# Fifteen shared units among the convolution steps, fourteen ahead of the experts, eleven behind them

## The chip, the core and the metric

The kernel runs on one core of one Trainium2 chip. The metric is device time in microseconds (us) of one execution. TensorE (PE) multiplies, VectorE (DVE), ScalarE (ACT) and GpSimd (POOL) do the rest of the arithmetic, and SyncE (SP) issues most transfers. The program is written in blocks, one for each engine: each engine does its instructions in the order in which its block has them, and semaphores tie the blocks together.

## What is computed

x is 16 x 128 x 256. A layer with a long convolution (gated by `ctx_2048`) adds to x, then a mixture of 32 experts (4 for each token, with a shared expert beside them) adds to the sum. Cut to its core:

```python
x = x + tanh(g_xattn) * xattn(ctx, ctx, layernorm(x))    # kv = k_i * v_j by head; y = conv(kv, ssm_kernel) + D*kv; out = sum_i y * q_i
inp = layernorm(x)
xn = w_norm * rmsnorm(inp)                               # 2048 tokens x 256
probs = softmax(xn @ w_router); w_topk, sel = top_k(probs, 4)
buf[e, pos] = xn[token]                                  # up to 128 rows for each of 32 experts
y = (silu(buf @ w_gate) * (buf @ w_up)) @ w_down         # inner width 176
out[token] += y[e, pos] * w_topk
sh = silu(xn @ sw_gate) * (xn @ sw_up) @ sw_down         # the shared expert, inner width 704
out = out + sigmoid(xn @ w_shared_gate) * sh
x = x + tanh(g_ffn) * (inp + out)
```

## The kernel before, in words

**Stages.** The 16 sequences are worked on in 4 groups of 4 (`G`, `GB`). The convolution of a group takes 8 steps (`NP_`, two heads each): VectorE and POOL form products, TensorE convolves (`conv`, L1040), VectorE multiplies and reduces (`mult`, `reduce`, L788). While the steps of group g run, the tokens of group g-1 get their norm, router logits, top 4 and slots, a chain through TensorE (`out_tr`, `xn_transposes`, `logits`, `rank`), ScalarE (`token_rows`, `xn_evac`, `lg_copy`, `exps`, `token_coef`, `base_rows`) and VectorE (`x1`, `token_stats`, `token_shift`, `top`, `top_masks`, `token_slots`, `token_gates`). POOL then sends the rows of the tokens to their experts' buffers (L396, 64 sends). The chain of the last group has no convolution beside it; it is written out by itself on every engine. When all rows are sent, SyncE loads the experts' inputs (L313); the 32 experts follow (TensorE L1204 to L1255, with ScalarE and VectorE between its products); POOL adds their results into three sums in DRAM (L470). In the tail SyncE loads the sums, VectorE adds them to `x_sb` (`add_sum`, L987 to L1018, 24 additions of 128 x 512), and ScalarE's queue stores the output.

**Shared units.** The shared expert of the 4 groups is cut into 40 units (`unit(n)`, L1101), 10 for a group: 5 full units (`gate`, `up`, six products of 128 x 512 each), one remainder (`gate` alone, six products, since 704 is 5 times 128 and 64 more) and 4 downs (`down`, L1086, six products each of 128 x 256). Unit n is number n % 10 of group n // 10: 0 to 4 are full, 5 is the remainder, 6 to 9 are downs. A unit of the first two kinds needs a `silu` on ScalarE (L538) and a `use` on VectorE (L791: the product of the two halves, L798 or L800), and a down needs only a `use` (L806: it adds to `x_sb`). There are single PSUM tiles `pg` and `pu` for them: the next gate waits for the silu before, the next up for the use before, and a down of number 2 or 3 for the use of an earlier down. The first gate of a group waits for the uses of all downs of the group before it, and for the low part of the group's tokens (`xnT_low`). The first down of a group waits for the use of its remainder.

**Where the units stand.** Units 0 to 17 stand among the convolution steps, by the table `UNIT_AT` (L45): unit `UNIT_AT[g, p]` comes on TensorE behind the convolution of step (g, p+1), on ScalarE at step (g, p) (behind `token_rows` of p = 2, behind the first `xn_evac` of p = 3, between `lg_copy` and `exps` of p = 4), and its use on VectorE ahead of the reduction of step (g, p). `LATE = 18` (L48) is the first of the units ahead of the experts: 18 to 31 stand in the last chain and behind it (TensorE L1191 to L1202, ScalarE L664 to L674, VectorE L943 to L960). `UNITS_END = range(32, 40)` (L50) are those behind the experts. On VectorE their uses are woven into the tail: in a loop of four one `add_sum` of sum 2, a use, another `add_sum` (L1002 to L1005), then the 16 additions of sums 0 and 1 (L1011 to L1018), then the four last uses.

## Time and profile before

| | before |
|---|---|
| median of 3 runs | 321.08 us (318.03, 321.08, 321.09) |
| profiled execution | 319.66 us, its span 317.9 us |
| PE busy | 275.6 us, 87% |
| PEld (weight loads, beside PE) busy | 224.8 us, 71% |
| DVE busy | 204.1 us, 64% |
| POOL busy | 192.0 us, 60% |
| ACT busy | 122.7 us, 39% |

The busy shares are averages over the span. The kernel has stages with different limits (to 78 us loads and the first two groups, to 158 us groups 2 and 3, to 206 us the last chain and the sends, to 287 us the experts, then the tail), so a share says little of what an edit in one stage is worth. The chain that ended last names, for each piece of the time, the engine or transfer that was waited for; the timeline of an engine gives the start and length of each run of equal instructions and, in brackets, how long the engine was idle just before and what ended that wait; the windows give busy time and the granted TensorE clock (PEclk, 1.00 is 2.4 GHz, 0.50 is 1.2 GHz) of a stretch.

### The profile page before, as it was taken

What the parts mean: (1) busy time and instruction counts of PE and PEld (TensorE: products, weight loads), DVE (VectorE), ACT (ScalarE), POOL (GpSimd) and SP (SyncE); (2) the same over time, 40 slices, a digit from 0 to 9 for tenths busy, and PEclk for the clock granted to TensorE, in tenths of its full rate; (3) what the DMA queues carried; (4) which work ended last, traced back from release to release, by engine and by line L of the source; (5) the groups of instructions that cost most, each with busy time, mean ns of one, the idle gap of its engine ahead of it and who ended that gap; (6) DMA issues with size and microseconds to landing.
All of it is one profiled execution on the core that took longest, in us unless ns stands there. A gap on an engine that the chain in (4) does not pass through costs nothing.

```text
span 317.9 us, 4992 instructions
## 1 busy us (share of the span) xinstructions
PE 275.6 (87%) x1482; PEld 224.8 (71%) x1482; DVE 204.1 (64%) x586; ACT 122.7 (39%) x342; POOL 192.0 (60%) x265
## 2 busy tenths in 40 slices
PE   2978659947998989899699999899999999999980
PEld 1877549835887868798477777677777777778750
DVE  2679999747769998688953621134554445555695
ACT  2248436871365701349115920143334333321100
POOL 2898977535689867686377677107655666652200
PEclk9979997968999999999979999999999999999996
DMA  6899999998112112011059930409999999668798
GB/s 203 246 301 292 302 269 386 384 299 234 56 42 72 61 53 74 37 65 45 4 174 284 236 102 0 132 20 241 252 260 259 256 290 295 104 114 234 165 354 306
DMA packets 53322, 59.65 MB, mean 188 GB/s; under 512 B 6744, under 2 KB 48920, under 8 KB 53296
## 3 DMA queue, kind: packets, MB, share of 16 engines
q1 hardware_dynamic: 42336, 47.24, 48.9%
q0 software_dynamic: 7680, 8.95, 14.3%
q10 hardware_dynamic: 3280, 3.15, 2.9%
q8 instruction: 12, 0.20, 0.2%
q14 instruction: 14, 0.11, 0.1%
HBM read 36.83 MB, written 27.21 MB: 201 GB/s over the span
## 4 chain that ended last, share of the span: by engine, by line
PE 42%; DVE 18%; SPq 15%; DMA 12%; ACT 6%; issue 5%; POOL 1%; DVEq 0%; ACTq 0%; POOLq 0%
PE Y L1220 12%; DMA arena<-in_ctx_dram 5%; SPq L300 5%; PE pg L1065 5%; DVE arena L788 4%; PE pd L1239 4%; DMA expert_sum<-arena,ide 4%; PE Y L1239 4%; SPq L290 4%; SPq L296 3%; PE pu L1065 3%; DVE x_sb L989 3%; PE Y L1211 2%; PE pm L1230 2%; PE pg L1098 2%
## 5 line engine op out<-in xcount | busy, mean ns | idle before, releaser
L396 POOL DMA_INDIRECT dispatched<-rows,dsu x64 | 63.4, 990 | 31.5 <-issue 23.9
L470 POOL DMA_INDIRECT expert_sum<-arena,ide x32 | 49.6, 1550 | 46.8 <-DVE arena L979 39.2
L788 DVE TENSOR_REDUCE arena<-arena 128x128 f32<-128x1024 f32 x32 | 38.7, 1212 | 0.2
L1053 PE MATMUL Y<-arena 128*128 128x144 f32 x128 | 28.3, 304 | 11.5 <-DVE arena L780 11.0
L966 DVE TENSOR_TENSOR arena<-arena,Y 128x176 f32<-128x176 f32 x32 | 10.8, 338 | 37.6 <-ACT arena L688 37.6
L798 DVE TENSOR_TENSOR act<-silu,pu 128x512 f32<-128x512 f32 x20 | 13.7, 686 | 31.5 <-PE pu L1065 17.5
L1053 PEld LDWEIGHTS Y<-arena 128*128 128x128 f32 x128 | 20.8, 196 | 15.8 <-issue 12.3
L681 ACT ACTIVATE arena<-Y,wn 128x128 f32<-128x128 f32 x64 | 20.0, 364 | 29.6 <-PE Y L1211 29.5
L547 ACT ACTIVATE silu<-pg 128x512 f32<-128x512 f32 x20 | 11.9, 595 | 48.9 <-PE pg L1065 48.8
L1055 PE MATMUL Y<-arena 128*128 128x144 f32 x128 | 26.7, 291 | 0.0
L1054 PE MATMUL Y<-arena 128*128 128x144 f32 x128 | 26.7, 291 | 0.0
L1065 PE MATMUL pg<-xnT_high,swgu_high 128*128 128x512 f32 x48 | 20.9, 435 | 5.8 <-ACT silu L547 5.0
L1220 PE MATMUL Y<-arena 128*128 128x352 f32 x72 | 24.3, 460 | 0.0
L1098 PE MATMUL pu<-swd,act 128*128 128x256 f32 (+1 forms) x84 | 21.8, 403 | 0.0
L1098 PE MATMUL pg<-swd,act 128*128 128x256 f32 (+1 forms) x84 | 21.2, 393 | 0.0
L1054 PEld LDWEIGHTS Y<-arena 128*128 128x128 f32 x128 | 20.7, 196 | 0.0
L1055 PEld LDWEIGHTS Y<-arena 128*128 128x128 f32 x128 | 20.6, 195 | 0.0
L384 POOL TENSOR_TENSOR arena<-arena 128x256 f32<-128x256 f32 x32 | 20.5, 642 | 0.0
L1065 PE MATMUL pg<-xnT_high,swgu_low 128*128 128x512 f32 x48 | 19.3, 402 | 0.0
L1065 PE MATMUL pg<-xnT_low,swgu_high 128*128 128x512 f32 x48 | 19.2, 401 | 0.0
L1220 PE MATMUL Y<-first_slots,arena 128*128 128x352 f32 x56 | 18.9, 460 | 0.0
L1098 PEld LDWEIGHTS pu<-swd,act 128*128 128x128 f32 (+1 forms) x84 | 15.6, 198 | 4.5 <-issue 2.7
(180 smaller groups left out, 653.3 us busy)
## 6 DMA issues: line engine op xcount, KB each, us to landing
expert_sum<-zrow SPq DMA_DIRECT2D x3, 2176.0 KB, 17.5
dispatched<-zrow SPq DMA_DIRECT2D x1, 4624.0 KB, 21.1
arena<-dispatched SPq DMA_DIRECT2D x32, 144.5 KB, 4.1
arena<-expert_sum SPq DMA_DIRECT2D x16, 256.0 KB, 5.8
arena<-in_L_ffn_w_gate_dram SPq DMA_DIRECT2D x18, 176.0 KB, 3.7
arena<-in_L_ffn_w_up_dram SPq DMA_DIRECT2D x18, 176.0 KB, 4.7
arena<-in_L_ffn_w_down_dram SPq DMA_DIRECT2D x18, 176.0 KB
first_slots<-in_L_ffn_w_gate_dram SPq DMA_DIRECT2D x14, 176.0 KB, 4.0
```

The source lines that it names most:

```text
L384: pool.tensor_tensor(o[:, :, :, 5:9], k[:, :, 0:4].rearrange("m e (u t) -> m e u t", t=1).broadcast_to([P, 16, 4, 4]), k[:, :, 4:8].rearra ...
L396: pool.indirect_dma_start(buf, bass.IndirectOffsetOnAxis(ap=dsu[:, t % 2, j:j + 1], axis=0), rows[:, t % 2, j // K, :], None, bounds_check ...
L470: pool.indirect_dma_start(accs[a], bass.IndirectOffsetOnAxis(ap=ide[:, e % NO:e % NO + 1], axis=0), ye[:, e % NO, :], None, compute_op=ALU ...
L681: ins = act_e.activation(xeT[:, e % 2, c, :], xt_out(e)[:, c * P:(c + 1) * P], ACT.Copy, scale=wn[:, c:c + 1])
L788: dve.tensor_reduce(oT[:, g % 2, :, 2 * HD * p:2 * HD * (p + 1)].rearrange("l e (a j) -> l a e j", a=2), Z[:, p % 2].rearrange("l (a e) j ...
L1053: pe.matmul(yv[:, 0], TT[:, h, P:L], kvv[:, 0], start=True, stop=True)
L1054: pe.matmul(yv[:, 1], TT[:, h, 0:P], kvv[:, 0], start=True, stop=False)
L1055: ins = pe.matmul(yv[:, 1], TT[:, h, P:L], kvv[:, 1], start=False, stop=True)
L1065: ins = pe.matmul(out_, swgu[a][:, c, col:col + P], xnT[b][:, gs % 2, c, :], start=(k == 0), stop=(k == n - 1))
L1098: ins = pe.matmul(down_out(gs, b), act[0:w, j, b * S:(b + 1) * S], swd[0:w, j, :], start=(j == 0), stop=(j == NJ - 1))
L1220: ins = pe.matmul(gu_out(e), xeT[:, e % 2, c, :], wgu[slot_of(e)][:, :, c, :], start=(c == 0), stop=(c == 1))
L1239: ins = pe.matmul(y_out(e), aeT[:, e % 2, c, :], wd[slot_of(e)][:, c, :], start=(c == 0), stop=(c == 1))
```

## The change

The table has units 0 to 14 at steps (2, 1) to (3, 7) in place of 0 to 17 at (1, 6) to (3, 7). `LATE` is 15, and `UNITS_END` is 29 to 39. So three units leave the convolution steps, and these are, in number, two downs and one remainder; the 14 units ahead of the experts are now 15 to 28 (a remainder and four downs of group 1, the whole of group 2 but its last down), and 29, a down of group 2, stands behind the experts with all ten of group 3. In the last chain ScalarE does the silu of unit 15 ahead of the token rows, and `last_exps` comes at once behind `lg_copy`, where a silu stood between; VectorE's uses there are of the remainder and of downs; TensorE no longer puts gates and ups between the transposes, the logits and the rank, but downs. In the tail, VectorE uses unit 29 first, then does the pairs of sum 2 with the uses of 30 to 33 behind each pair, then the uses of 34 and 35, then the 16 additions and the last four uses.

```diff
--- before.py
+++ after.py
@@ -42,12 +42,11 @@
 LN_EPS, RMS_EPS = 1e-5, 1e-6
 
 
-UNIT_AT = {(1, 6): 0, (1, 7): 1,
-           (2, 0): 2, (2, 1): 3, (2, 2): 4, (2, 3): 5, (2, 4): 6, (2, 5): 7, (2, 6): 8, (2, 7): 9,
-           (3, 0): 10, (3, 1): 11, (3, 2): 12, (3, 3): 13, (3, 4): 14, (3, 5): 15, (3, 6): 16, (3, 7): 17}
-LATE = 18
+UNIT_AT = {(2, 1): 0, (2, 2): 1, (2, 3): 2, (2, 4): 3, (2, 5): 4, (2, 6): 5, (2, 7): 6,
+           (3, 0): 7, (3, 1): 8, (3, 2): 9, (3, 3): 10, (3, 4): 11, (3, 5): 12, (3, 6): 13, (3, 7): 14}
+LATE = 15
 WARM = 10
-UNITS_END = range(32, 40)
+UNITS_END = range(29, 40)
 
 
 def flamingo_block(nc, x, ctx_in, g_xattn, g_ffn, ssm_kernel, ssm_D, w_norm, w_router, w_gate, w_up,
@@ -658,16 +657,14 @@
                             q_stats(g + 2)
 
             t = G - 1
+            silu(LATE)
             token_rows(t)
             xn_evac(t, 0)
             xn_evac(t, 1)
-            silu(LATE + 2)
             lg_copy(t)
+            last_exps(t)
             for c in range(2):
                 xn_high(t, c)
-            silu(LATE + 3)
-            last_exps(t)
-            silu(LATE + 4)
             token_coef(t)
             base_rows(t)
             for n in range(LATE + 5, UNITS_END[0]):
@@ -948,12 +945,12 @@
             use(LATE)
             token_shift(t)
             use(LATE + 1)
+            use(LATE + 2)
             top(t)
             shift(t)
             top_masks(t)
-            use(LATE + 2)
+            use(LATE + 3)
             token_slots(t)
-            use(LATE + 3)
             token_gates(t)
             last_low(t)
             for k in range(LATE + 4, UNITS_END[0]):
@@ -997,12 +994,15 @@
                 if e + 1 < E:
                     e_aT(e + 1)
                 e_yout(e)
+            use(UNITS_END[0])
             dve.wait_ge(s["base_ready"], G)
             dve.wait_ge(s["down_used"], GB * (G - 1))
             for k in range(G):
                 pair_mark[0, 2 * k] = mark(add_sum(2, 2 * k))
-                use(UNITS_END[k])
                 pair_mark[0, 2 * k + 1] = mark(add_sum(2, 2 * k + 1))
+                use(UNITS_END[k + 1])
+            for k in UNITS_END[G + 1:-GB]:
+                use(k)
 
             def add_first(i):
                 after(pair_mark[0, i])
@@ -1190,14 +1190,12 @@
             out_tr(t, 1)
             unit(LATE)
             unit(LATE + 1)
+            unit(LATE + 2)
             xn_transposes(t, 0)
             xn_transposes(t, 1)
-            gate(2, 0)
             logits(t)
-            up(2, 0)
-            gate(2, 1)
+            unit(LATE + 3)
             rank(t)
-            up(2, 1)
             for n in range(LATE + 4, UNITS_END[0]):
                 unit(n)
```

The first place is ScalarE at the end of group 1 and the start of group 2 (`vq`, `rqs`, `nbq` are the query's coefficients, `arena` the queries and keys of later steps, `silu` the unit's result out of `pg`). Before:

```order
L521 ACTIVATE vq<-qss 128x4
L547 ACT_TABLE_LOAD
L547 ACTIVATE silu<-pg 128x512
L525 ACTIVATE rqs<-rq 128x4
L527 ACTIVATE nbq<-nmq,rq 128x1 x4
L499 ACTIVATE arena<-x_sb,nbq,rqs 128x2x128
L547 ACTIVATE silu<-pg 128x512
L484 ACTIVATE arena<-pd 128x2x8x16
L492 ACTIVATE arena<-pd 128x2x16x8
L499 ACTIVATE arena<-x_sb,nbq,rqs 128x2x128
L547 ACTIVATE silu<-pg 128x512
L484 ACTIVATE arena<-pd 128x2x8x16
```

Now:

```order
L520 ACTIVATE vq<-qss 128x4
L524 ACTIVATE rqs<-rq 128x4
L526 ACTIVATE nbq<-nmq,rq 128x1 x4
L498 ACTIVATE arena<-x_sb,nbq,rqs 128x2x128
L483 ACTIVATE arena<-pd 128x2x8x16
L491 ACTIVATE arena<-pd 128x2x16x8
L498 ACTIVATE arena<-x_sb,nbq,rqs 128x2x128
L483 ACTIVATE arena<-pd 128x2x8x16
L491 ACTIVATE arena<-pd 128x2x16x8
L498 ACTIVATE arena<-x_sb,nbq,rqs 128x2x128
L546 ACT_TABLE_LOAD
L546 ACTIVATE silu<-pg 128x512
```

The silus of units 0, 1 and 2 stood between the coefficients and the queries and keys of the group, with the table load of the first; now the first silu, unit 0's, comes behind four query and key steps.

The second place is VectorE in the last chain (`x_sb<-pu` and `x_sb<-pg` are uses of downs, `act` a use of a full unit or of the remainder, `mx` to `M` the top 4, `rk` the first step of the slots). Before:

```order
L838 TENSOR_SCALAR vs<-mv 128x4
L806 SCALAR_TENSOR_TENSOR x_sb<-pu,sgf,x_sb 128x256
L844 SCALAR_TENSOR_TENSOR nb<-mv,rs 128x4
L806 SCALAR_TENSOR_TENSOR x_sb<-pg,sgf,x_sb 128x256
L852 MAX mx<-lg 128x8 x4
L870 TENSOR_TENSOR ex<-lg,mx 128x128
L859 COPY top<-mx 128x4x4
L861 MATCH_REPLACE left<-top,lg 128x36 x4
L866 TENSOR_TENSOR M<-left,lg 128x128
L798 TENSOR_TENSOR act<-silu,pu 128x512
L897 TENSOR_TENSOR rk<-pm,carry 128x128
```

Now:

```order
L835 TENSOR_SCALAR vs<-mv 128x4
L797 TENSOR_TENSOR act<-silu,pg 64x512
L841 SCALAR_TENSOR_TENSOR nb<-mv,rs 128x4
L803 SCALAR_TENSOR_TENSOR x_sb<-pu,sgf,x_sb 128x256
L803 SCALAR_TENSOR_TENSOR x_sb<-pg,sgf,x_sb 128x256
L849 MAX mx<-lg 128x8 x4
L867 TENSOR_TENSOR ex<-lg,mx 128x128
L856 COPY top<-mx 128x4x4
L858 MATCH_REPLACE left<-top,lg 128x36 x4
L863 TENSOR_TENSOR M<-left,lg 128x128
L803 SCALAR_TENSOR_TENSOR x_sb<-pu,sgf,x_sb 128x256
L894 TENSOR_TENSOR rk<-pm,carry 128x128
```

The use of the remainder is new in this place, ahead of `nb`, and a use of a down (`x_sb<-pu`, unit 18) stands where the use of a full unit (`act`, unit 20) stood, ahead of the slots.

The third place is VectorE in the tail (`x_sb<-x_sb,arena` are the additions of the sums, `act` the uses of full units and, 64 wide, of the remainder; the rest are uses of downs). Before:

```order
L989 TENSOR_TENSOR x_sb<-x_sb,arena 128x512
L798 TENSOR_TENSOR act<-silu,pu 128x512
L989 TENSOR_TENSOR x_sb<-x_sb,arena 128x512 x2
L798 TENSOR_TENSOR act<-silu,pu 128x512
L989 TENSOR_TENSOR x_sb<-x_sb,arena 128x512 x2
L798 TENSOR_TENSOR act<-silu,pu 128x512
L989 TENSOR_TENSOR x_sb<-x_sb,arena 128x512 x2
L800 TENSOR_TENSOR act<-silu,pg 64x512
L989 TENSOR_TENSOR x_sb<-x_sb,arena 128x512 x17
L806 SCALAR_TENSOR_TENSOR x_sb<-pu,sgf,x_sb 128x256
L806 SCALAR_TENSOR_TENSOR x_sb<-pg,sgf,x_sb 128x256
L806 SCALAR_TENSOR_TENSOR x_sb<-Y,sgf,x_sb 128x256 x2
```

Now:

```order
L803 SCALAR_TENSOR_TENSOR x_sb<-pg,sgf,x_sb 128x256
L986 TENSOR_TENSOR x_sb<-x_sb,arena 128x512 x2
L795 TENSOR_TENSOR act<-silu,pu 128x512
L986 TENSOR_TENSOR x_sb<-x_sb,arena 128x512 x2
L795 TENSOR_TENSOR act<-silu,pu 128x512
L986 TENSOR_TENSOR x_sb<-x_sb,arena 128x512 x2
L795 TENSOR_TENSOR act<-silu,pu 128x512
L986 TENSOR_TENSOR x_sb<-x_sb,arena 128x512 x2
L795 TENSOR_TENSOR act<-silu,pu 128x512 x2
L797 TENSOR_TENSOR act<-silu,pg 64x512
L986 TENSOR_TENSOR x_sb<-x_sb,arena 128x512 x16
L803 SCALAR_TENSOR_TENSOR x_sb<-pu,sgf,x_sb 128x256
```

A use of a down has come ahead of the first addition, two more uses of full units lie ahead of that of the remainder, and all sums but the first eight additions are behind it (16 now, 17 before).

## Rows read from the trace of the kernel before

**Rows 1.** Page, chain that ended last: shares of the span by engine

```profile
PE 42%; DVE 18%; SPq 15%; DMA 12%; ACT 6%; issue 5%; POOL 1%; DVEq 0%; ACTq 0%; POOLq 0%
```

**Rows 2.** Chain of waits to 78 us: start, us, what

```profile
69.92 8.07 DMA arena<-in_ctx_dram
```

**Rows 3.** Windows: stretch, length, busy us (instructions) by engine, PEclk, DMA share, GB/s

```profile
78.00:120.00 42.00, 39.61 (x247) 33.86 (x248) 34.82 (x95) 18.71 (x49) 33.22 (x53) 1.00 0.17 60
...
158.00:206.00 48.00, 45.00 (x209) 34.73 (x210) 18.32 (x62) 15.91 (x34) 31.08 (x31) 0.96 0.56 151
```

**Rows 4.** Timeline of PE, 60 to 130 us: start, us, what, [idle before, releaser]

```profile
68.31 0.79 PE L1065 MATMUL pg<-xnT_high,swgu_high 128*128 128x512 f32 x1 [4.18 <-ACT silu L547]
...
73.53 0.41 PE L1053 MATMUL Y<-arena 128*128 128x144 f32 x2
...
78.04 0.44 PE L1031 MATMUL pd<-ident,arena 128*128 128x128 f32 x2 [1.72 <-DMA arena<-in_ctx_dram]
...
78.46 0.48 PE L1065 MATMUL pg<-xnT_high,swgu_high 128*128 128x512 f32 x1
...
81.29 0.60 PE L1117 MATMUL pm<-ident,arena 128*128 128x128 f32 x4
...
96.93 0.48 PE L1053 MATMUL Y<-arena 128*128 128x144 f32 x2 [1.20 <-DVE arena L780]
...
118.14 0.48 PE L1053 MATMUL Y<-arena 128*128 128x144 f32 x2 [1.14 <-DVE arena L780]
```

**Rows 5.** Timeline of PE, 130 to 208 us

```profile
158.71 1.10 PE L1117 MATMUL pm<-ident,arena 128*128 128x128 f32 x4 [2.57 <-DVE arena L788]
...
200.39 0.47 PE L1065 MATMUL pg<-xnT_high,swgu_high 128*128 128x512 f32 x1 [0.81 <-DVE x_sb L806]
...
205.97 0.39 PE L1211 MATMUL Y<-ident,arena 128*128 128x128 f32 x2
```

**Rows 6.** Timelines of POOL, DVE and SP's queue, 70 to 202 us

```profile
74.37 1.22 POOL L396 DMA_INDIRECT dispatched<-rows,dsu  x1 [5.37 <-issue]
...
179.79 1.33 POOL L396 DMA_INDIRECT dispatched<-rows,dsu  x1 [1.58 <-DVE rows L888]
...
175.46 0.29 DVE L897 TENSOR_TENSOR rk<-pm,carry 128x128 f32<-128x128 f32 x1 [0.27 <-PE pm L1147]
...
178.98 1.29 DVE L876 TENSOR_TENSOR xnT_low<-xnT,xnT_high 128x512 fp32r<-128x512 f32 x2
...
201.50 12.39 SPq L313 DMA_DIRECT2D arena<-dispatched  x9
```

**Rows 7.** Timeline of all engines in the tail, 278 to 318 us

```profile
287.05 0.59 PE L1065 MATMUL pg<-xnT_high,swgu_high 128*128 128x512 f32 x1
...
289.98 0.39 PE L1065 MATMUL pg<-xnT_high,swgu_high 128*128 128x512 f32 x1
...
295.42 0.39 PE L1065 MATMUL pg<-xnT_high,swgu_high 128*128 128x512 f32 x1
...
296.79 2.94 PE L1098 MATMUL pu<-swd,act 128*128 128x256 f32 x12
...
297.62 0.69 DVE L800 TENSOR_TENSOR act<-silu,pg 64x512 f32<-64x512 f32 x1
...
301.12 2.04 DVE L989 TENSOR_TENSOR x_sb<-x_sb,arena 128x512 f32<-128x512 f32 x3 [2.09 <-DMA arena<-expert_sum]
...
303.41 9.53 DVE L989 TENSOR_TENSOR x_sb<-x_sb,arena 128x512 f32<-128x512 f32 x13 [0.25 <-DMA arena<-expert_sum]
...
312.97 0.48 DVE L806 SCALAR_TENSOR_TENSOR x_sb<-pu,sgf,x_sb 128x256 f32<-128x256 f32 x1
```

**Rows 8.** Windows of 1 us around 68 and 159: columns as in rows 3

```profile
68.00:69.00 1.00, 0.69 (x2) 0.60 (x3) 0.71 (x2) 1.00 (x6) 1.00 (x3) 0.50 0.91 252
...
159.00:160.00 1.00, 1.00 (x6) 1.00 (x5) 0.20 (x2) 0.00 (x0) 0.94 (x1) 0.50 0.18 56
```

## Prediction, made before the changed kernel ran

> **What bounds the kernel now.** I read the chain that ended last first: TensorE has the largest share, VectorE less than half of that, and SyncE's queue and the transfers about a quarter together [rows 1]. So no engine is the bound throughout, and I went on by stages, with cuts where the chain changes hands.
>
> To 78.0 us the chain is SyncE's queue and then one transfer, the context of the last group, which TensorE waits for at 78.04 [rows 2, 4]. Nothing that is computed before that sets the end. From 78 to 158.7 (groups 2 and 3 of the convolution) TensorE is busy 39.6 of the first 42 us [rows 3]; its few waits are for VectorE [rows 4], which was itself held by a use that came behind ScalarE's token rows. From 158.7 to 206.0 two paths run side by side and end together: POOL's 32 row sends with the first expert load behind them (201.50), and TensorE's shared units; TensorE is busy 45.0 of 48 us and starts the experts at 205.97, at once after its last unit [rows 3, 5, 6]. The experts follow at TensorE's pace to 287.05. In the tail TensorE has four gate/up units and four downs left, but VectorE has the last word: it ends its uses at 298.3, adds one piece, then waits 2.09 us for the expert sums, and adds 16 pieces from 301.12 to 312.94 with hardly a gap [rows 7].
>
> **Prices.** A full unit (gate and up, 12 products) takes 2.72 us (289.98 to 295.42 is two), the remainder unit 1.37, a down product 2.94 [rows 7]. A use is 0.6 to 0.7 us, after a down 0.5.
>
> **The work that moves.** The convolution steps lose one remainder and two downs: 7.3 us. Ahead of the experts two full units go and one down and one remainder come: 1.1 us less. Behind them two full units and one down come: 8.4 us more. The count is the same in all, so only what each stage does with its share matters.
>
> *Up to 78 us: nothing, and a price.* Units 0 and 1 stood ahead of 73.5 [rows 4]. Without them the end of this stage is still the transfer. But TensorE then has only one convolution step and the first transposes of group 1's output left. VectorE, no longer held by unit 0, hands these over some 5 us earlier (as long as POOL now waits for VectorE's slots at 74.37 [rows 6]), so TensorE has nothing from about 69 to 78. What that does to its clock is in the rows: after 4.18 us of waiting the granted clock was 0.50 (1.2 GHz), and the unit that began at 68.31 took 5.2 us to the next instruction, against 2.83 at 78.46 [rows 4, 8]. After 2.57 us of waiting at 158.71 the clock was again 0.50 [rows 5, 8], while the unit behind the 1.72 us of 78.04 ran at full pace [rows 4]. With 9 us idle I expect 1.2 GHz at 78, for about as long as from 68.31 on: 2.3 us lost, the 5.2 less 2.8. Bounds: 0 if it recovers at once, 4 if it takes twice as long. The Trainium skill (TensorE: Matmul & The Clock Gate, section "What's actually happening") says that the slow clock is the default and that activity releases it; by that rule the two moved units were what kept it awake, and the trace agrees, with 0.50 after both waits. By it this term is the 2.3 above; for a clock that did not ask for activity it would be 0.
>
> A second price: the first group's sends on POOL wait for slots which VectorE delivers late, because it stood behind unit 0. They would begin about 5 us ahead of 74.37 [rows 6], so about three more of them share the transfer engines before 78. I take 0, bound +1.5 us.
>
> *Group 2, 78 to 118.1.* Its first step loses a full unit (78.46 to 81.29, 2.8 us). Steps 1 and 2 keep full units. Step 3 gets a full unit for the remainder, 1.4 us more, but ended in 1.20 us of waiting [rows 4], so 0. Steps 4 and 5 get a full unit for a down: 0.2 less each. Step 6 gets the remainder for a down: 1.6 less. Step 7 stays. Sum -4.8; with the wait of 1.14 at 118.14 gone too it would be -5.9, and if VectorE, which has 34.8 of 42 us of work here, becomes the pace, about -3. With the slow clock: -4.8 + 2.3 = -2.5.
>
> *Group 3, 118.1 to 158.7.* Three downs and five full units replace five full, one remainder and two downs: 1.6 us more. The steps with downs have no silu, so that VectorE's wait behind ScalarE's rows (the same that stood in group 2) falls away, and the end of the group is VectorE's ranking and its last two reductions, not the last unit. I take 0, bounds -1.6 and +1.6.
>
> *The last chain, 158.7 to 206.* TensorE's list gets 1.1 us shorter. Of its waits of before, 0.8 at 200.39 and as much before another gate disappear [rows 5]. New: the logits have no gate product ahead of them, so about 1 us passes while ScalarE empties the transposes. And unit 20 must wait for the use of unit 19, which on VectorE stands behind the ranking and the two low parts. Counted from the end of the logits, TensorE is free after two downs and the rank, 6.3; VectorE needs the down of unit 18 (2.9), a use (0.5), slots and gates (175.46 to 178.98 less one use, 2.9), the low parts (1.2) and a use (0.5; all [rows 6]), and the gate starts 0.3 later: 8.3. So 2 us of idle, after which the clock may fall once more (0 to 1.7, as at 158.71). Sum: -1.1 - 1.6 + 1.0 + 2.0 = +0.3, with the clock up to +2.0; if the waits hide, -2.4. POOL's sends gain at most 0.5 here, since the rows of the last group are ready, with the exponentials out of the way, no earlier than VectorE's ranking, and POOL waited only 1.58 for them [rows 6]. I take 0.
>
> So the experts begin 2.5 us earlier (bounds 0 and -6). Beyond about -5.5 the first expert load would set the start: it is issued when the sends have landed, 4.5 us ahead of the first transpose [rows 5, 6], and these come forward by 4.8 and 0.5 at most.
>
> *Experts*: the same instructions at the same pace, 0.
>
> *Tail.* Counted from 287.05, where unit 32 begins now. TensorE first does unit 29, a down: 2.9. Then unit 30's gate waits for its use, as the gate at 200.39 waited for a use, 0.8 [rows 5]. Five full units 13.6: the remainder starts at +17.4 (now +8.4). VectorE's use of the remainder starts 2.2 behind that now (295.42 to 297.62) and takes 0.7: it ends at +20.3. Only then, in VectorE's order, come the 16 adds, which began at +14.1. The sums have landed by then (now the last wait for them is at 303.41, +16.4), so the adds take 11.7 (9.53 for 13) without a wait: to +32.0 instead of +25.9, 6.1 later. The four downs end on TensorE at +30.6, before that, so they are hidden. The four last uses (1.7) and the last store follow as now. The stores no longer share the engines with the sums, at most 0.4 off the last landing. I take +6.1, bounds +5.5 and +6.6.
>
> **Sum.** -2.5 + 6.1 = +3.6 us. The profiled execution took 319.66 us (span 317.9, 1.8 around it), so 323.3 for it; it lay 1.4 below the median of the runs, 321.08, to which the same sum gives **324.7 us**, 1.1% slower.
>
> **Rivals.** *The early gain pays for the tail* (no change, the other side). If the clock does not fall at 78, or comes back after the first transposes, and the wait ahead of unit 20 hides, the experts begin 5 to 6 us earlier, where the first expert load stops it: -6 + 6.1, 321.2 us. For it: TensorE at full clock is the pace of groups 2 and 3. Against it: the two rows at 0.50. It decides from 3 us of early gain on (the tail's 6.1 less 1% of the time).
> *The transfer of 78 lands later*, since the sends are moved ahead of it: 1.5 us more, +5.1, 326.2. For it: the transfer takes 8.07 us already, behind weights [rows 2]. Against it: SyncE issued it behind these weights, and few sends were under way.
> *The tail does not grow*, because the sums set the adds anyway. They do so today by 2.09 us, but the use moves by 9: without the growth 318.6 us, and 1% under the kernel before with a little more early gain. Nothing that is moved delays the sums by the 6 us that this would need.
> *A TensorE-paced dispatch with both clock dips at their full length*: no early gain, +6.1, 327.2.
>
> **How the numbers follow.** A measurement of this kernel can tell about 1% (3.2 us) from no change. My forecast with its range of +3 to +5 has 0.42, the late transfer 0.10, the two full dips 0.08; the early gain that pays (-1 to +3) 0.35, the tail that doesn't grow 0.05. Of the first three a part, 0.03, lies just under 1%; of the last nearly all, 0.04, I count as faster: slower 0.57, same 0.39, faster 0.04. The time is that of the likeliest. The range takes in +6.4 above and, below, most of the case in which the early gain pays: 320.0 to 327.5. The forecast's own range is 324.0 to 326.0.
>
> **What would show it.** TensorE idle from about 69 to 78 and then a granted clock of 0.50 for some microseconds; the second step's convolution hardly earlier than now although a unit is gone; the experts' first transpose at 203 to 204; about 2 us of idle ahead of unit 20; in the tail, 16 adds that begin 20 us after the last expert's down instead of 14, without a wait for a transfer, and a last down product that ends before the last add. I am wrong if the clock is whole at 78, if the first expert transpose comes before 202, or if VectorE still waits for sums in the tail.

## The result: 2.1% slower, and the profile after

The changed kernel took 327.12 us (median of 4 runs, 324.94 to 328.31), the kernel before 320.66 beside it (318.03 to 321.09); the ratio is 1.0211, with a 95% interval of 1.0131 to 1.0292. So it is slower, and whether by more than 2% is open. The forecast was 324.7 with a range of 320.0 to 327.5. The profiled executions are 8.1 us apart (spans 317.9 and 326.0). Cut where the prediction cut them:

| stretch | before | after | difference | predicted |
|---|---|---|---|---|
| start to the last group's first output transpose | 158.71 | 160.29 | +1.58 | -2.5 |
| from there to the first expert transpose | 47.26 | 50.00 | +2.74 | about 0 |
| experts, to the last one's down | 81.08 | 81.38 | +0.30 | 0 |
| tail, to the end | 30.85 | 34.33 | +3.48 | +6.1 |
| sum | 317.9 | 326.0 | +8.1 | +3.6 |

The chain that ended last, shares of the span by engine:

```profile
PE 58%; SPq 15%; DVE 13%; DMA 7%; issue 5%; ACT 1%; DVEq 0%; ACTq 0%
```

TensorE has 58% where it had 42% [rows 1]: of what ends last, more is TensorE's, though its busy time hardly changed (279.4 us for 275.6). The timeline of TensorE from 60 to 81 us, with start, length, what and the wait ahead, answers to [rows 4]:

```profile
67.64 0.66 PE L1117 MATMUL pm<-ident,arena 128*128 128x128 f32 x4 [1.31 <-DVE arena L785]
...
78.61 0.69 PE L1031 MATMUL pd<-ident,arena 128*128 128x128 f32 x2 [10.32 <-DMA arena<-in_ctx_dram]
...
80.38 0.69 PE L1053 MATMUL Y<-arena 128*128 128x144 f32 x2
```

TensorE is idle from 68.3 to 78.6, as predicted, and runs the transposes and the convolution behind it at half pace: two products of the convolution take 0.69 where they took 0.41 [rows 4]. Windows of 1 us (columns as in rows 3) show the granted clock here and at three more places:

```profile
81.00:82.00 1.00, 1.00 (x6) 1.00 (x5) 0.96 (x4) 0.00 (x0) 0.00 (x0) 0.50 0.00 0
...
115.00:116.00 1.00, 1.00 (x6) 1.00 (x6) 0.91 (x6) 0.00 (x0) 0.00 (x0) 0.50 0.00 0
...
173.00:174.00 1.00, 1.00 (x7) 1.00 (x6) 0.00 (x0) 0.00 (x0) 0.83 (x1) 0.50 1.03 328
...
187.00:188.00 1.00, 1.00 (x4) 0.81 (x3) 0.00 (x0) 0.42 (x1) 0.70 (x2) 0.50 0.00 0
```

It is 0.50 until 83, again at 114 to 117, again from 172 to 179, and at 186 to 189. Of these only the first and the last were forecast. The timeline of TensorE around 114 and in the last chain:

```profile
108.32 0.48 PE L1053 MATMUL Y<-arena 128*128 128x144 f32 x2 [0.96 <-DVE arena L777]
...
113.86 0.54 PE L1053 MATMUL Y<-arena 128*128 128x144 f32 x2 [2.00 <-DVE arena L777]
...
116.59 3.44 PE L1098 MATMUL pu<-swd,act 128*128 128x256 f32 x12
...
160.29 0.66 PE L1117 MATMUL pm<-ident,arena 128*128 128x128 f32 x4 [2.10 <-DVE arena L785]
...
171.34 2.82 PE L1134 MATMUL pm<-wr,xnT 128*128 128x33 f32 x16 [0.97 <-ACT xnT L567]
...
173.97 5.47 PE L1098 MATMUL pu<-swd,act 128*128 128x256 f32 x12
...
179.37 0.22 PE L1143 MATMUL pm<-M,tri 128*128 128x32 bf16 x2
...
184.79 0.47 PE L1065 MATMUL pg<-xnT_high,swgu_high 128*128 128x512 f32 x1 [2.02 <-DVE x_sb L803]
...
210.29 0.50 PE L1209 MATMUL Y<-ident,arena 128*128 128x128 f32 x2
```

In group 2 TensorE waits for VectorE, 0.96 and 2.00 us, and a down then takes 3.44. In the last chain it waits 0.97 us at the logits, the clock falls, the logits take 2.82 (1.94 with TensorE awake, below) and the down of unit 18 takes 5.47 (3.03). The ranking stands behind it, at 179.37, 8.0 us after the logits began; it came 4.5 us after them before. What hangs on the ranking, on POOL and SyncE's queue, answers to [rows 6]:

```profile
183.65 1.33 POOL L395 DMA_INDIRECT dispatched<-rows,dsu  x1 [4.40 <-DVE rows L885]
...
206.25 12.08 SPq L312 DMA_DIRECT2D arena<-dispatched  x9
```

The sends of the last group wait 4.40 us for VectorE's rows, and the first expert load is issued at 206.25 instead of 201.50. TensorE's list ends at 210.29, 4.04 after that load; before the two lay 4.47 apart. So both paths came late together, and TensorE, which comes there without a wait for the load, came last. The tail, all engines, answers to [rows 7]:

```profile
291.67 2.95 PE L1098 MATMUL pg<-swd,act 128*128 128x256 f32 x12
...
295.40 0.47 PE L1065 MATMUL pg<-xnT_high,swgu_high 128*128 128x512 f32 x1 [0.78 <-DVE x_sb L803]
...
311.28 0.69 DVE L797 TENSOR_TENSOR act<-silu,pg 64x512 f32<-64x512 f32 x1 [1.22 <-ACT silu L548]
...
312.00 9.72 DVE L986 TENSOR_TENSOR x_sb<-x_sb,arena 128x512 f32<-128x512 f32 x16
...
316.32 6.04 PE L1098 MATMUL Y<-swd,act 128*128 128x256 f32 x24
...
321.76 0.48 DVE L803 SCALAR_TENSOR_TENSOR x_sb<-pu,sgf,x_sb 128x256 f32<-128x256 f32 x1
```

The order is the forecast one: a down, a wait of 0.78 for its use, five full units and the remainder, whose use begins 19.6 us behind the start; the 16 additions begin at +20.3, without any wait. But they take 9.72, not 11.7, and TensorE's last down ends at 322.36, later than the last addition (321.72).

### The profile page after: what moved, and what is told of

Read it like the earlier page. It is cut to its first block, busy times and chain, and to the rows that moved or that the text cites. A ratio compares the mean times of both kernels' runs of the same rounds, so it can differ in the third digit from the quotient of the medians.

```text
span 326.0 us, 4992 instructions
## 1 busy us (share of the span) xinstructions
PE 279.4 (86%) x1482; PEld 229.3 (70%) x1482; DVE 204.2 (63%) x586; ACT 122.7 (38%) x342; POOL 192.2 (59%) x265
## 4 chain that ended last, share of the span: by engine, by line
PE 58%; SPq 15%; DVE 13%; DMA 7%; issue 5%; ACT 1%; DVEq 0%; ACTq 0%
PE Y L1218 12%; PE pg L1065 8%; PE pu L1065 7%; DMA arena<-in_ctx_dram 5%; PE pu L1098 5%; SPq L289 4%; PE pd L1237 4%; PE Y L1237 4%; SPq L299 4%; PE pg L1098 4%; SPq L295 3%; DVE arena L785 3%; PE Y L1209 2%; PE pm L1228 2%; PE Y L1053 2%
## 5 line engine op out<-in xcount | busy, mean ns | idle before, releaser
L1053 PE MATMUL Y<-arena 128*128 128x144 f32 x128 | 29.3, 313 | 15.0 <-DVE arena L777 13.9
L1053 PEld LDWEIGHTS Y<-arena 128*128 128x128 f32 x128 | 21.5, 203 | 18.9 <-issue 14.4
L1054 PE MATMUL Y<-arena 128*128 128x144 f32 x128 | 27.9, 302 | 0.0
L1055 PE MATMUL Y<-arena 128*128 128x144 f32 x128 | 27.9, 302 | 0.0
L1098 PE MATMUL pu<-swd,act 128*128 128x256 f32 (+1 forms) x84 | 23.8, 430 | 0.6 <-DVE act L797 0.6
L1065 PE MATMUL pg<-xnT_high,swgu_high 128*128 128x512 f32 x48 | 20.0, 416 | 2.8 <-DVE x_sb L803 2.8
L1054 PEld LDWEIGHTS Y<-arena 128*128 128x128 f32 x128 | 21.7, 205 | 0.0
L1055 PEld LDWEIGHTS Y<-arena 128*128 128x128 f32 x128 | 21.6, 204 | 0.0
L1098 PEld LDWEIGHTS pu<-swd,act 128*128 128x128 f32 (+1 forms) x84 | 17.2, 216 | 6.0 <-issue 2.6
## 6 DMA issues: line engine op xcount, KB each, us to landing
expert_sum<-zrow SPq DMA_DIRECT2D x3, 2176.0 KB, 17.2
```

What stands on the lines that cost most here:

```text
L1053: pe.matmul(yv[:, 0], TT[:, h, P:L], kvv[:, 0], start=True, stop=True)
L1054: pe.matmul(yv[:, 1], TT[:, h, 0:P], kvv[:, 0], start=True, stop=False)
L1055: ins = pe.matmul(yv[:, 1], TT[:, h, P:L], kvv[:, 1], start=False, stop=True)
L1065: ins = pe.matmul(out_, swgu[a][:, c, col:col + P], xnT[b][:, gs % 2, c, :], start=(k == 0), stop=(k == n - 1))
L1098: ins = pe.matmul(down_out(gs, b), act[0:w, j, b * S:(b + 1) * S], swd[0:w, j, :], start=(j == 0), stop=(j == NJ - 1))
```

## The experiments

Every run is compared with the kernel before on the same chip. The kernel before itself spreads by up to 1.9% there, and the transposes that wait for the context of the last group begin at 75.4 to 79.5 us in these traces, so stretches are counted from these transposes, or from the last group's output transposes, rather than from the start.

### The tail part alone

```diff
-UNITS_END = range(32, 40)
+UNITS_END = range(29, 40)
...
+            use(UNITS_END[0])
...
                 pair_mark[0, 2 * k] = mark(add_sum(2, 2 * k))
-                use(UNITS_END[k])
                 pair_mark[0, 2 * k + 1] = mark(add_sum(2, 2 * k + 1))
+                use(UNITS_END[k + 1])
+            for k in UNITS_END[G + 1:-GB]:
+                use(k)
```

> The kernel before with only one part of the change: units 29 to 31 go from ahead of the experts to behind them, with the tail of the change on VectorE; the convolution steps and the last chain stay as they were. Theory (the sends on POOL and the first expert load set the start of the experts, and the tail costs what the profile after shows): TensorE's list ahead of the experts is 8.4 us shorter, but the first expert transpose still comes at 205.5 to 206, with TensorE idle ahead of it by about 8 us; the tail grows by 3.5 us (34.3 from the last expert's down to the end, where it was 30.9), so 324 to 325 us. Rival (TensorE's list sets the start): the experts begin at 198 to 200, 6 to 8 us earlier, and the whole is 3 to 5 us faster than before, 316 to 318 us. Second rival (the cold clock after 8 us of idle slows the first experts too): 326 us or more.

Ratio 1.0156 (1.0125 to 1.0187). TensorE's timeline at the start of the experts and behind them:

```profile
201.94 0.70 PE L1214 MATMUL Y<-ident,arena 128*128 128x128 f32 x2 [7.12 <-DMA arena<-dispatched]
...
286.03 2.95 PE L1101 MATMUL pg<-swd,act 128*128 128x256 f32 x12
```

TensorE waits 7.12 us for the first load: the sends set the start, and the three units taken from ahead of the experts bought only 2.5 us (44.8 from the output transposes to the first expert transpose, 47.3 before). The tail is 34.4 us from 286.03 to the span's end at 320.4, the same 3.5 us longer as in the whole change. And the idle time has a price of its own: the granted clock is 0.50 from 199 to 208, over the first three experts, and the experts take 84.1 (201.94 to 286.03) for 81.1; 2.8 of these 3.0 are lost by the fourth expert's transposes. The first theory holds on the tail and on who sets the start; the second rival, which it did not exclude, adds the 3.0. The start came at 201.9, below the 205.5 expected, by the 2.5 us and because this execution was 1.55 us ahead at the output transposes.

### TensorE kept awake at 78

```diff
                     if p == 0:
                         out_tr(t, 0)
+                    if p == 0 and g == 2:
+                        for i in range(76):
+                            pe.transpose(pg[:, 0:P], ident[:], ident[:])
```

> The changed kernel with 76 transposes of the identity, about 9 us of filling work, on TensorE ahead of the transposes that wait for the context of the last group; nothing reads them. Theory (the low clock behind the idle time from 68 to 78 costs 2.4 us of group 2): the granted clock is 1.00 from 78 on, the third step of group 2 (fourth convolution) starts at 84 to 84.5 where it was 86.6, and since VectorE paces the last three steps of the group, 1 to 2.4 us of that arrive at the end of group 3, 158 to 159 where it was 160.3; the whole 325 to 326.5 us. Rival (VectorE paces all of group 2, so the clock costs nothing): the end of group 3 stays at 160.3 and the time within 0.5 us of the change.

Ratio 1.0111 (1.0072 to 1.0151). From the first transpose behind the context to the last group's output transposes it takes 75.6 us (77.68 to 153.28), the change 81.7 (78.61 to 160.29), the kernel before 80.7. So in these executions the clock at 78 was worth 6.1 us, more than twice the 2.4 expected. By the two ratios the whole gained less, 1.0% or 3.2 us; the profiled execution of the change is the second slowest of its four. The first 2.4 are where they were looked for: from the transpose to the fourth convolution of the group it takes 5.5 us for 8.0. The rest is VectorE's. Its timeline in the change, then POOL's at the same time, then VectorE's with TensorE awake (M is the mask of the chosen experts, `rows` their gates):

```profile
102.11 2.96 DVE L863 TENSOR_TENSOR M<-left,lg 128x128 bf16<-128x128 f32 x1
...
108.29 1.79 DVE L885 SCALAR_TENSOR_TENSOR rows<-ex,tg,esum 128x128 f32<-128x128 f32 x1
...
102.08 0.41 POOL L376 TENSOR_TENSOR arena<-arena 128x128 f32<-128x128 f32 x1
...
103.64 1.27 POOL L406 TENSOR_TENSOR xnT_low<-xnT,xnT_high 128x512 fp32r<-128x512 f32 x1
...
98.99 0.38 DVE L863 TENSOR_TENSOR M<-left,lg 128x128 bf16<-128x128 f32 x1
...
103.15 0.35 DVE L885 SCALAR_TENSOR_TENSOR rows<-ex,tg,esum 128x128 f32<-128x128 f32 x1
```

The mask takes 2.96 us in the change: it ends at 105.07, when POOL's run of products and the low part (102.08 to 104.91) is over; the gates take 1.79. With TensorE awake they take 0.38 and 0.35. These 4 us are what TensorE then waits for, 0.96 and 2.00, and behind the 2.00 its clock falls a second time. With TensorE awake there is no wait ahead of the first of these convolutions, 0.18 ahead of the second and 1.29 ahead of the next one (where the change has none), and the clock stays whole. Both theories of the expectation were too small: the low clock had shifted VectorE's steps onto POOL's products. How much hangs on this meeting, the run with the ranking first shows below.

### The ranking ahead of unit 18

```diff
-            unit(LATE + 3)
             rank(t)
+            unit(LATE + 3)
...
-            use(LATE + 3)
             token_slots(t)
             token_gates(t)
+            use(LATE + 3)
```

> The changed kernel with the ranking product ahead of unit 18 on TensorE, and the use of unit 18 behind slots and gates on VectorE. Theory (the dispatch was late because the ranking stood behind a down product that the low clock stretched to 5.4 us, and the slots behind its use): the logits end at 174.0 as in the change, the ranking starts at 176.5 where it was 179.4, the sends of the last group start at 180.5 to 181 where it was 183.65, and the first expert load is issued at 203 to 203.5 where it was 206.25. TensorE waits 2.5 us for the ranking and does two downs after it, so its own list ends at 210 to 211 and the experts start at 210: the whole within 1 us of the change. Rival (VectorE's order alone delays the sends): the sends start at 182.5 or later. Rival (TensorE was waiting for VectorE all along, so that the earlier slots help its unit 20): the experts start at 207 to 208 and the whole is 2 to 3 us faster than the change.

Ratio 1.0224 (1.0163 to 1.0285), the change's 1.0211 within it. TensorE's timeline from the logits on, and POOL's first send of the last group:

```profile
170.76 2.82 PE L1134 MATMUL pm<-wr,xnT 128*128 128x33 f32 x16 [0.97 <-ACT xnT L567]
...
176.11 0.21 PE L1143 MATMUL pm<-M,tri 128*128 128x32 bf16 x2 [2.53 <-DVE M L863]
...
176.48 5.63 PE L1098 MATMUL pu<-swd,act 128*128 128x256 f32 x12
...
209.80 0.50 PE L1209 MATMUL Y<-ident,arena 128*128 128x128 f32 x2
...
180.40 0.97 POOL L395 DMA_INDIRECT dispatched<-rows,dsu  x1 [1.72 <-DVE rows L885]
```

The ranking starts 5.35 us behind the start of the logits (8.0 in the change), the sends at 180.40 and the first load at 201.90 (183.65 and 206.25). But TensorE waited 2.53 us for the mask, unit 18 takes 5.63 all the same, and the first expert transpose comes 50.1 us behind the output transposes, 50.0 in the change. So the sends alone were not it: TensorE's list, at the low clock, is as late. The first theory holds.

### A unit ahead of the wait, in the kernel before

```diff
+                    if (g, p) == (2, 0):
+                        unit(UNIT_AT[g, p])
                     if p < 4 and g + 1 < G:
                         k_tr(g + 1, p)
...
-                    if (g, p) in UNIT_AT:
+                    if (g, p) in UNIT_AT and (g, p) != (2, 0):
```

> The kernel before with one unit moved on TensorE alone: unit 2 stands ahead of the transposes that wait for the context of the last group, not behind them. Theory (work that lies ahead of that transfer is free, and TensorE's list from 78 on sets the end of groups 2 and 3 and of the last chain): unit 2 runs from 74.4 to 77.5, the next convolution starts at 79 where it was 81.7, and 2 to 2.8 us of it arrive at the start of the experts, 203.5 to 204; the whole 2 to 2.8 us faster than before. Rival (VectorE paces the end of group 2): the gain is gone by the step at 118 and the time is as before. Rival (the transposes of the last group come later, since the unit ends after the transfer): up to 0.5 us slower.

Ratio 1.0004 (0.9958 to 1.0049). The convolution of step 2 starts at 79.88 (81.73 before), but then:

```profile
90.69 0.48 PE L1053 MATMUL Y<-arena 128*128 128x144 f32 x2 [0.95 <-DVE arena L780]
...
96.68 0.48 PE L1053 MATMUL Y<-arena 128*128 128x144 f32 x2 [1.20 <-DVE arena L780]
...
90.64 2.07 ACT L559 ACTIVATE rows<-x_sb,nb,rs 128x256 f32<-128x256 f32 x4 [2.65 <-DVE nb L844]
...
93.33 0.69 DVE L798 TENSOR_TENSOR act<-silu,pu 128x512 f32<-128x512 f32 x1 [2.72 <-ACT silu L547]
```

These are TensorE's waits and, below, ScalarE's rows of the tokens and VectorE's use of the silu that comes behind them. VectorE is only 0.25 us ahead of the kernel before from its use at 81.31 on (81.56 there), so TensorE waits 0.95 at 90.69; then the use of the silu behind the rows holds VectorE for 2.72, as it did before, and TensorE waits 1.20. The gain is 0.25 by the step at 96.7. The rival holds: in the kernel before, work taken from TensorE alone in group 2 is worth nothing while a full unit stands behind the token rows.

### TensorE kept awake everywhere

```diff
 (the 76 transposes at 78, and)
             t = G - 1
+            for i in range(12):
+                pe.transpose(pd[:, 0:P], ident[:], ident[:])
             out_tr(t, 0)
...
+            for i in range(6):
+                pe.transpose(Y[:, 0, 0:P], ident[:], ident[:])
             logits(t)
...
+                if n == 2 * UNITS:
+                    for i in range(14):
+                        pe.transpose(Y[:, 0, 0:P], ident[:], ident[:])
                 unit(n)
```

> The changed kernel with filling transposes at every place where TensorE waited: 76 ahead of the context's wait (as in the run before), 12 ahead of the last group's output transposes, 6 ahead of the logits, 14 ahead of unit 20; nothing reads them. Theory (the last chain of the change costs 2.7 us more than before because the clock falls behind the 0.97 us wait at the logits and stretches them and unit 18, which stands ahead of the ranking, and again at unit 20): the granted clock stays 1.00 from 78 to the experts, the logits take 1.9 us and unit 18 3.0, the ranking comes 4.5 to 5 us behind the start of the logits where it came 8.0, the first expert load and the experts come 4.5 to 5 us earlier than in the kernel with only the 76 transposes (203.3), at 198 to 199; the tail stays at 34.3; the whole 315 to 317 us, 1 to 1.5% under that kernel. Rival (waits for VectorE and ScalarE pace the last chain, so that a faster clock only lengthens the waits): the last chain stays above 48 us and the experts begin at 201.5 or later.

Ratio 0.9945 (0.9882 to 1.0008): 2.6% under the change by the two ratios. Windows of groups 2 and 3 and of the last chain (columns as in rows 3), and the logits and the ranking on TensorE:

```profile
78.00:152.00 74.00, 72.09 (x451) 62.13 (x449) 60.34 (x183) 36.26 (x91) 54.43 (x80) 1.00 0.15 51
...
152.00:198.00 46.00, 44.08 (x224) 34.68 (x224) 18.68 (x63) 15.42 (x33) 30.98 (x31) 1.00 0.54 152
...
163.69 1.94 PE L1134 MATMUL pm<-wr,xnT 128*128 128x33 f32 x16 [0.31 <-ACT xnT L567]
...
165.47 3.03 PE L1098 MATMUL pu<-swd,act 128*128 128x256 f32 x12
...
168.43 0.21 PE L1143 MATMUL pm<-M,tri 128*128 128x32 bf16 x2
```

The clock is whole all the way; the ranking comes 4.7 us behind the start of the logits, and the last chain takes 45.1 us (152.63 to 197.73) for 50.0 in the change and 50.1 with only the first filling. The rival, that waits would take the gain, falls. The tail keeps its 34.4 us. The interval of the ratio reaches 1.0008, so against the kernel before this is no clear gain.

### The same with the ranking first

```diff
             logits(t)
-            unit(LATE + 3)
+            for i in range(18):
+                pe.transpose(Y[:, 0, 0:P], ident[:], ident[:])
             rank(t)
+            unit(LATE + 3)
...
```

> The same with the ranking product ahead of unit 18 and the use of unit 18 behind slots and gates, 18 filling transposes ahead of the ranking and 6 ahead of unit 20. Theory (with a whole clock the order of ranking and unit 18 moves the sends by 1 to 2 us but TensorE's list sets the start of the experts, so the order is worth nothing): sends of the last group start 1 to 2 us earlier than in the other, experts at the same time within 0.5 us, the whole within 0.3%. Rival (the sends and the first load set the start once TensorE is fast): experts 1 us or more earlier.

Ratio 1.0037 (0.9943 to 1.0131), the interval of the other reaching over it. The last chain takes 46.6 us (155.55 to 202.11), 1.5 more than with unit 18 ahead; the sends of the last group begin 19.8 us behind the output transposes, 20.1 in the other. So the order gains the sends 0.2 us, not 1 to 2, since both wait for VectorE, and costs TensorE what the filling holds. Unit 18 was good cover for the mask, as long as it takes 3 us.

The same run tests the price of the low clock at 78. Here the 76 transposes ended before the context came:

```profile
78.69 0.69 PE L1031 MATMUL pd<-ident,arena 128*128 128x128 f32 x2 [2.63 <-DMA arena<-in_ctx_dram]
...
101.29 0.29 DVE L863 TENSOR_TENSOR M<-left,lg 128x128 bf16<-128x128 f32 x1
...
101.40 0.44 POOL L376 TENSOR_TENSOR arena<-arena 128x128 f32<-128x128 f32 x1
```

The clock fell behind the wait of 2.63, to 0.50 from 78 to 82. But groups 2 and 3 took 76.9 us (78.69 to 155.55), only 1.2 more than with TensorE awake. The mask began 0.11 us ahead of POOL's products and took 0.29; in the change it began 0.03 behind them and took 2.96. (The fall itself was shorter too: 1.6 us lost by the fourth convolution, where the change lost 2.4.) So of the 6.1 us at most about 2.4 are the low clock itself, and most of the rest came from a meeting that a tenth of a microsecond decides. The run with the ranking first but without filling has the same code as the change up to there, met POOL in the same way (a mask of 2.95) and took 81.8.

### Units 0 and 1 where they were

```diff
-UNIT_AT = {(2, 1): 0, (2, 2): 1, ... (2, 7): 6, (3, 0): 7, ... (3, 7): 14}
+UNIT_AT = {(1, 6): 0, (1, 7): 1, (2, 1): 2, ... (2, 7): 8, (3, 0): 9, ... (3, 5): 14}
```

> The changed kernel with its 15 units in other places of the convolution: units 0 and 1 at steps 6 and 7 of group 1, as before the change, 2 to 8 at steps 1 to 7 of group 2, 9 to 14 at steps 0 to 5 of group 3, none at the last two steps; no filling. Theory (units 0 and 1 kept TensorE's clock whole at 78 and cost nothing there): the granted clock is 1.00 from 78 on, the convolution of step 2 of group 2 starts near 79, group 2 ends at 113.5 to 114.5 as with the filling transposes, and group 3, with six units for eight, ends at 149 to 151 where that kernel had 153.3; the last chain takes 50 as in the change; experts at 199 to 201, the whole 316 to 318 us. Rival (the clock is low at 78 all the same, since TensorE also waits there): (2,3) starts at 86 and group 3 ends above 155. Rival (VectorE, with the uses of units 0 and 1 ahead of the first group's slots, paces group 2): group 2 ends at 117 or later.

Ratio 1.0088 (1.0026 to 1.0151), 1.2% under the change. Group 2 took 37.5 us from the context's transposes to the second convolution of group 3 (77.44 to 114.89), 41.4 in the change and 35.5 with the filling. But group 3 did not get shorter with two units less, 39.8 us, and at its end:

```profile
154.65 1.11 PE L1117 MATMUL pm<-ident,arena 128*128 128x128 f32 x4 [7.31 <-DVE arena L786]
```

TensorE waits 7.31 us for VectorE. Group 3 took 40.6 us before, 40.3 in the change and 40.1 with TensorE awake at 78, with very different units in it: VectorE sets its length. The clock fell at 78 here too, behind a wait of 2.22, for about 3 us, and again within the wait at the end, at 150, until 161. So the first theory holds in that the two units cost nothing ahead of 78; it is wrong on the clock and on group 3, and the experts came at 201.8, not at 199 to 201. The kernel before waits 1.72 at 78 and has a unit behind the wait; which of the two kept its clock whole was not tried. The last chain took 47.2 us, not 50: behind the same wait of 0.97 at the logits the clock stayed whole.

### The kernel before, awake at 158

```diff
             t = G - 1
+            for i in range(18):
+                pe.transpose(pd[:, 0:P], ident[:], ident[:])
             out_tr(t, 0)
```

> The kernel before with 18 filling transposes ahead of the last group's output transposes, where TensorE waits 2.57 us and the clock then is at 0.50 for 3.5 us. Theory (this fall costs about 1.7 us, the 1.7 of the two transposes and the 3.8 of the down behind them less what they take at full clock, and lies on both paths of the last chain, the sends and TensorE's list): the clock stays 1.00, the logits come 1 to 1.7 us earlier after the output transposes, the experts begin 1 to 1.7 us earlier, the whole 1 to 1.7 us under the kernel before. Rival (POOL's sends behind each other set the start): POOL's wait of 1.58 for the rows shrinks, the load is issued at most 1 us earlier, and the whole is within 0.5 us of the kernel before.

Ratio 1.0127 (1.0065 to 1.0189): slower, which neither theory expected. The timeline of TensorE, and windows (columns as in rows 3):

```profile
158.90 0.66 PE L1117 MATMUL pm<-ident,arena 128*128 128x128 f32 x4 [0.46 <-DVE arena L788]
...
167.59 0.75 PE L1126 MATMUL pm<-ident,rows 128*128 128x128 f32 x4 [1.83 <-ACT rows L561]
...
171.29 2.19 PE L1134 MATMUL pm<-wr,xnT 128*128 128x33 f32 x16
...
162.00:166.00 4.00, 3.76 (x15) 2.41 (x14) 2.06 (x12) 0.63 (x2) 3.13 (x3) 1.00 0.89 249
...
169.00:171.00 2.00, 2.00 (x6) 1.51 (x6) 0.00 (x0) 0.66 (x2) 1.47 (x2) 0.50 1.06 285
```

The output transposes and the downs run at full clock now. For that very reason TensorE is done with the downs earlier and waits longer for the token rows, 1.83 us where it waited 0.68; behind this wait the clock falls, from 168.5 to 172, and now it falls on the unit ahead of the logits and on the logits. The logits start 12.4 us behind the output transposes (11.7 before), the ranking 17.2 (16.2), the experts 48.2 (47.3). So 0.9 of the 4 us are shown. The two profiled executions are only 1.3 apart (spans 319.2 and 317.9), so no trace shows the rest, and it stays open.

### Awake at both waits

```diff
 (the 18 transposes above, and)
+            for i in range(16):
+                pe.transpose(Y[:, 0, 0:P], ident[:], ident[:])
             xn_transposes(t, 0)
```

> The kernel before with filling transposes at both places of the last chain where TensorE waited in the run with one filling: 18 ahead of the output transposes and 16 ahead of the token transposes; nothing reads them. Theory (in the run with one filling the low clock was not gone but came behind the next wait, 1.83 us, and there fell on the logits that the ranking waits for): the granted clock is 1.00 from 158 to 206, the logits start 11.0 to 11.4 us behind the output transposes (12.4 with one filling, 11.7 before), and the experts 45.3 to 46.3 behind them (48.2 with one filling, 47.3 before); the whole 1 to 2 us under the kernel before. Rival (the filling itself delays the chain, by holding TensorE when the rows are ready): the experts come 47 us or more behind the output transposes and the whole is no faster than before.

Ratio 0.9945 (0.9909 to 0.9980). Window of the last chain:

```profile
158.00:204.00 46.00, 44.42 (x221) 34.34 (x220) 17.10 (x60) 15.91 (x34) 30.11 (x30) 1.00 0.58 156
```

The clock is whole; the logits start 11.15 us behind the output transposes and the experts 46.7. The chain gained 0.5 of the 1 to 2 us on the kernel before and 1.5 on the run with one filling, and the whole is 1.8 us under the kernel before. So the fall had moved in the run above. The gain stands at the logits, 0.5 earlier; from them to the experts it is 35.6 us here and before. The sends do not bound this: TensorE comes to the first expert transpose without a wait for the load, which was issued 4.4 us earlier, while 2.2 us were enough where only the tail part was changed.

### A version drawn from this, with and without filling

Both have units 0 and 1 at steps 6 and 7 of group 1, 2 to 16 at the 15 places of the change, 14 units ahead of the experts in the manner of the kernel before with a third down (19) ahead of the token transposes, and 9 behind the experts. The first has 20 filling transposes ahead of the context's wait and 12 ahead of the last output transposes.

> A version drawn from the runs: units 0 and 1 at steps 6 and 7 of group 1, where TensorE has nothing else, 2 to 16 at the 15 places of the change, 14 units ahead of the experts as before the change, 9 behind them; three downs (17 to 19) cover the wait for the token rows, then gates and ups stand between logits and ranking as before; 20 filling transposes ahead of the context's wait and 12 ahead of the last output transposes. Theory (VectorE paces groups 2 and 3, so which units stand there matters little, and TensorE's clock and list set the rest): the clock is 1.00 from 78 on, group 3 ends 75 to 76 us behind the context, at 153 to 154, the experts begin 44 to 45.5 later, at 197 to 199, the tail takes 31 to 32, the whole 311 to 313.5 us, 1.3 to 2% under the kernel before. Rival (the clock falls at another wait): experts at 200 or later, the whole 315 or more. Rival (VectorE, held by the uses of units 0 and 1, lets the last group's context be used late): group 3 ends above 156.

> The same without any filling transposes. Theory (the 32 filling transposes are what keeps the clock whole at 78 and at the last output transposes): the clock falls at one or both places, groups 2 and 3 or the last chain are 2 to 4 us longer, the whole 313.5 to 317 us. Rival (the units alone keep TensorE busy enough): within 0.3% of the version with fillings.

With filling the ratio is 0.9893 (0.9840 to 0.9945), the lowest of all, though its interval meets those of the two other filled versions at 0.9945; without it 0.9981 (0.9950 to 1.0013). Both are slower than expected: 315.6 us for 311 to 313.5, and 318.2 for 313.5 to 317. With filling:

```profile
99.52 1.92 DVE L859 COPY top<-mx 128x16 f32<-128x16 f32 x1
...
157.36 0.66 PE L1120 MATMUL pm<-ident,arena 128*128 128x128 f32 x4 [1.86 <-DVE arena L788]
...
202.92 0.51 PE L1221 MATMUL Y<-ident,arena 128*128 128x128 f32 x2 [0.34 <-DMA arena<-dispatched]
```

The clock is whole from 78 on. The last chain takes 45.6 us and ends with a wait for the first load, so the sends bound it. Groups 2 and 3 took 77.9 us, not the 75 to 76 expected; TensorE waits for VectorE in them (1.81 at 106.19). Two of VectorE's steps are late there, while POOL's products run: the copy of the top values takes 1.92 us (0.22 in the change) and a step of the slots 1.75 (0.29). Without filling the clock stayed whole at 78, unlike the theory, and fell at 115.9 and at 156.9; the last chain took 47.1. The mask takes 2.10 and the gates 1.68 in it, with no fall of the clock ahead of them: other shifts than a low clock lead to such a meeting too.

## Why the prediction was right, and where it was wrong

**The sign was right and the time lies in the range, but the sum is right partly by luck: two terms were wrong in opposite directions.** The early part was to gain 2.5 us and lost 4.3 (160.29 - 158.71 + 2.74), 6.8 off; the tail was to lose 6.1 and lost 3.5, 2.6 off. The measured 327.12 is 0.4 below the top of the range and outside the 324.0 to 326.0 of the forecast proper. Of its signs, the experts' first transpose at 203 to 204 did not come (210.29), nor did a last down that ends before the last addition.

**Up to 78.** Right as forecast: idle from 68 to 78, the clock at 0.50 behind it, and 2.3 us for it: by the fourth convolution of group 2 the change is 0.15 behind, of which 0.57 is a later transfer, so -0.4; the forecast's -2.8 and +2.3 give -0.5 (its own 5.2 less 2.8 is 2.4, not 2.3).

**Group 2.** The step that failed is the price of the low clock, 2.3 with bounds 0 and 4. The bounds held for the fall itself, and the sum without it was right: with TensorE awake the two groups take 75.6 us, 5.1 less than before, for a forecast -4.8. What was missing is that a low clock does not only cost its own time: here it moved VectorE's mask and gates onto POOL's products, TensorE then waited for VectorE, and its clock fell again. The price was 6.1, of which 2.4 stood by the fourth convolution and 3.1 in the steps of the two waits. Where the mask just missed POOL's products, a fall at 78 cost 1.2. VectorE as the pace had been a bound of the same paragraph ("about -3"), but only as a smaller gain.

**Group 3.** Right, 0 for a measured -0.2, and for the reason given: it is VectorE's.

**The last chain.** The wait ahead of unit 20 was forecast at 2.0 and measured 2.02, with a fall of the clock behind it, 1.6 us (unit 20 takes 4.35 for 2.72). The step that failed is the count of "two downs and the rank, 6.3" at full clock: the wait at the logits was forecast at 1 us and measured 0.97, but nothing was said of the clock behind it. It fell there, and cost 0.9 on the logits and 2.4 on unit 18, and with them the ranking and the sends: the 6.3 measured 8.6 (from 174.16, the end of the logits, to 182.77, the end of unit 19). Against that stands the fall at 158 that did not happen in this execution, behind 2.10 us of waiting. Awake, the chain is 45.1: 2.2 less than before, the "if the waits hide, -2.4" of the forecast. The forecast worked out +0.3 for this stretch and took 0.

**The tail.** Right in its order and in the absence of a wait. Two sizes were off. An addition takes 0.61 us (9.72 for 16), not the 0.73 of [rows 7]: 13 in 9.53 held small waits for the sums as they landed, since 12 starts 0.6 apart and one of 0.69 make 7.9. That is 2.0 of the 2.6 too much; the rest is the last store, 2.6 us behind the last use where it was 3.3. And TensorE's four downs, called hidden at +30.6, end at +30.7, just behind the additions.

**The rivals.** "The early gain pays for the tail" is what the kernel with TensorE awake is: 0.5% under the kernel before, which is not clear of no change, with the experts 7.1 us earlier, counted from the context's transposes (120.8 for 127.9). Its condition, a clock that does not fall, was the right one, and it was not met. "Both clock dips at their full length", 327.2, came nearest in the number; there were four falls, not two. The transfer that lands later is not decided: the transposes behind it begin 0.57 us later in the change, but at 75.4 to 78.2 in six traces with units 0 and 1 in their old places and at 76.9 to 78.7 in four without.

## What to carry to other kernels

Take filler work out of a latency-bound stretch only after asking what clock the engine will have behind each wait that this opens: here the falls and what they shifted cost 11 us between two profiled executions (6.0 in the groups, 4.9 in the last chain), 8.5 by the two ratios. Closing one wait can move the fall to the next: in the kernel before, filling at one wait lengthened the last chain by 0.9 us and filling at both shortened it by 0.5. And take the price of an operation from a run of them in which nothing is waited for: a mean over a run that follows landing transfers has the transfers in it.

## What the runs showed of the hardware that was not expected

The granted clock went to 0.50 behind idle stretches as short as 0.97 us (at the logits of the change) and stayed at 1.00 behind others of 2.10 (at 160.29 of the same execution). In the first case TensorE had been idle 2.10 at 158, 0.62 at 165 and 0.97 at 170; so the length of the last wait alone does not tell. With units 0 and 1 where they were, it stayed at 1.00 behind the same 0.97 at the logits. Transposes that nobody reads, put into those waits, kept it at 1.00 from 78 to the experts, with 1.03, 0.80, 0.31 and 0.33 us of the filled waits left; where they ended 2.63 us before the context came, it fell. The Trainium skill (TensorE: Matmul & The Clock Gate, section "What's actually happening") puts the penalty of the ramp, in a passage on a kernel's first products, under 1% of a typical kernel's span; here four falls in mid-kernel cost 2.6% by the two ratios, because they lay on the path and delayed VectorE too.

An operation of VectorE of 0.29 us took 2.96 while POOL ran products and a subtraction one behind the other, and ended 0.16 us after them. The same mask in all thirteen traces: it takes 2.96, 2.95 and 2.10 in the three where it begins while these run, and 0.29 to 0.38 in the ten others. The Trainium skill (SBUF — State Buffer, section "🔬 SBUF: two separate sides") tells of a port pair that the two engines share and that one of them holds for a whole instruction while the other is blocked; the trace agrees, and shows more: the mask was held through five instructions of POOL in a row, not one. Not every meeting holds: the mask of an earlier group in the change began at 58.54, inside a product of POOL (58.25 to 58.65), and took 0.29.
